# Block norm and router norm from one set of moments, with the order of the side tasks moved

## What is computed

```
attn   = softmax(s1) - sigmoid(lambda) * softmax(s2)         # causal
attn   = attn / max(sum(|attn|), 1e-6)
r1     = x + (attn @ v) @ Wo.T
x1     = (r1 - mean(r1)) / sqrt(var(r1) + 1e-5)              # block norm
xh     = (x1 - mean(x1)) * rsqrt(var(x1) + 1e-5)             # router norm
xn     = xh * gamma + beta                                   # to router and experts
probs  = softmax((xn @ router_w.T) / 1.5); top 2 of 8
moe    = sum over the top 2 of probs_e * (silu(xn @ W1[e]) @ W2[e])
out    = norm((moe + x1) + x1)                               # two residuals: 2 * x1
```

## Time and profile before

| | |
|---|---|
| runs | 1205.65, 1209.85, 1212.59 us; median 1209.85 |
| the profiled execution | 1201.04 us, of which the span of the trace is 1199.3 |
| busy share of the span | POOL 79%, PE 77%, DVE 77%, ACT 71% |
| costliest lines | L680 ACT exponentials 539.2 us, L962 DVE maxima 424.6, L614 POOL subtraction 406.5, L610 POOL scaling 312.4 |
| transfers | 139.39 MB, mean 116 GB/s over the span |
| mean granted clock of TensorE | 0.86 of full |

### The profile page before, as it was taken

One profiled execution on the slowest core, in us unless ns is written; L12 is line 12 of the kernel. 1 busy time (PEld: TensorE's weight loads), 2 busy tenths in 40 slices (PEclk: granted clock), 3 DMA queues, 4 the chain that ended last, 5 costly groups with the idle time before them and its releaser, 6 DMA issues.

```text
span 1199.3 us, 27952 instructions
## 1 busy us (share of the span) xinstructions
PE 927.8 (77%) x8522; PEld 738.7 (62%) x8522; DVE 924.3 (77%) x2393; ACT 851.7 (71%) x2706; POOL 948.1 (79%) x1257
## 2 busy tenths in 40 slices
PE   2588787868898788967799688977799787959582
PEld 1355564647676567846677466756578576748582
DVE  1588898859997799968997799968997689946242
ACT  1598987669887777868787777878788777853140
POOL 3399999898878997899878998799878898793402
PEclk9577788669998898989898898979998788978797
DMA  3703400533246524382235623382244632245662
GB/s 115 156 1 91 104 2 14 136 110 109 78 125 161 159 69 128 111 234 71 85 106 144 192 72 118 99 236 73 85 125 125 182 92 79 81 130 172 214 194 72
DMA packets 117046, 139.39 MB, mean 116 GB/s; under 512 B 11042, under 2 KB 99490, under 8 KB 116898
## 3 DMA queue, kind: packets, MB, share of 16 engines
q1 hardware_dynamic: 112802, 129.21, 37.4%
q0 software_dynamic: 4096, 8.40, 2.4%
HBM read 107.81 MB, written 29.75 MB: 115 GB/s over the span
## 4 chain that ended last, share of the span: by engine, by line
POOL 34%; DVE 22%; PE 19%; issue 12%; ACT 6%; DMA 5%; SPq 2%; DVEq 0%; POOLq 0%; ACTq 0%
POOL exps L614 13%; POOL exps L610 11%; DVE neg_max L962 7%; POOL x_sorted_dram L630 4%; PE trans L1124 4%; ACT exps L680 4%; POOL y_back L639 3%; DVE abs_sum L972 3%; PE scores L1090 3%; PE side L1067 3%; PE side L1073 3%; POOL lam_l L604 1%; DVE stats L760 1%; DMA xg<-x_sorted_dram 1%; DVE hT L924 1%
## 5 line engine op out<-in xcount | busy, mean ns | idle before, releaser
L680 ACT ACTIVATE exps<-scores,neg_max 128x512 f32<-128x512 f32 (+3 forms) x1024 | 539.2, 541 | 74.8 <-DVE neg_max L962 72.7
L962 DVE TENSOR_REDUCE neg_max<-scores 128x1 f32<-128x512 f32 (+3 forms) x896 | 424.6, 526 | 79.4 <-PE scores L1092 75.1
L614 POOL TENSOR_TENSOR exps<-exps 128x512 f32<-128x512 f32 x320 | 406.5, 1270 | 26.7
L610 POOL TENSOR_SCALAR exps<-exps,inv_l,lam_l 128x512 f32<-128x512 f32 (+3 forms) x512 | 312.4, 616 | 59.1 <-DVE inv_l L953 42.1
L1124 PE MATMUL trans<-ident,exps 128*128 128x128 f32 x1280 | 242.6, 320 | 148.4 <-POOL exps L614 114.0
L1124 PEld LDWEIGHTS trans<-ident,exps 128*128 128x128 f32 x1280 | 161.4, 160 | 216.3 <-POOL exps L614 169.6
L1090 PE MATMUL scores<-stack 72*128 72x512 bf16 (+3 forms) x1024 | 279.9, 343 | 15.5 <-DMA stack<-parts_dram 14.9
L972 DVE TENSOR_REDUCE abs_sum<-exps 128x1 f32<-128x512 f32 (+3 forms) x448 | 224.6, 525 | 67.6 <-POOL exps L614 67.2
L687 ACT ACTIVATE diffT<-trans 128x512 f32<-128x512 f32 x320 | 194.4, 608 | 95.2 <-PE trans L1124 93.8
L680 ACT ACTIVATION_READ_ACCUMULATOR exps<-scores,neg_max 128x1 f32 x1024 | 226.1, 221 | 0.0
L1092 PE MATMUL scores<-causal_bf,ident_bf 128*128 128x128 bf16 x1024 | 215.4, 243 | 0.0
(11 more groups left out here) (142 smaller groups left out, 871.9 us busy)
## 6 DMA issues: line engine op xcount, KB each, us to landing
w_sb<-w_dram SPq DMA_DIRECT2D x120, 512.0 KB, 3.7
stack<-parts_dram SPq DMA_DIRECT2D x288, 96.0 KB
parts_dram<-parts SPq DMA_DIRECT2D x104, 128.0 KB, 2.4
xg<-x_sorted_dram SPq DMA_DIRECT2D x24, 256.0 KB, 3.6
y_sorted_dram<-y_sorted SPq DMA_DIRECT2D x24, 256.0 KB, 3.8
x_in<-x_dram SPq DMA_DIRECT2D x8, 256.0 KB, 4.6
x_res<-x_dram SPq DMA_DIRECT2D x8, 256.0 KB, 4.6
o_dram<-y_out SPq DMA_DIRECT2D x8, 256.0 KB, 2.2
```

Of the source, the lines that this page charges most:

```text
L610: nc.gpsimd.tensor_scalar(diff[:, ring, col:col + w], exps[:, ring, 1, col:col + w], inv_l2[:, i:i + 1], lam_l1[:, i:i + 1], ALU.mult, ALU ...
L614: nc.gpsimd.tensor_tensor(diff[:, ring, :], diff[:, ring, :], exps[:, ring, 0, :], ALU.subtract)\
L680: nc.scalar.activation(exps[:, ring, k, col:col + w], scores[:, c % 2, k, col:col + w], ACT.Exp, bias=neg_max[:, c % 2, k, i:i + 1], accum ...
L962: nc.vector.tensor_reduce(neg_max[:, c % 2, k, i:i + many], scores[:, c % 2, k, col:col + many * w].rearrange("p (i w) -> p i w", w=w), AX ...
```

## The change

One set of moments serves both norms. With m and v the mean and variance of a row of `r1`, `x1` has mean 0 and variance v / (v + e), so the router norm of `x1` is (r1 - m) * (v (1 + e) + e^2)^-0.5, and twice `x1` is (r1 - m) * ((v + e) / 4)^-0.5. POOL makes both bases with one scale-and-add each over 128x4 and raises them in one power over 128x8, in task `out_proj`. Tasks `norm1` and `norm2` become one task `norms` at slot 18, in which DVE writes `x1_twice` and then `xh`, both straight from `r1` with four TENSOR_SCALAR each; `x1` is no longer made, and its moments and the 128x512 doubling are gone. The wait for the scatters of the batch before now stands between the two groups. The third norm uses the same functions; its epsilon is added by a constant instead of from the tile `eps_row`.

The order is moved too: `abs_sum` is taken five slots after its chunk instead of four (`LAG_DEN` follows it), `sorted` goes from slot 44 to 42, turn 2 from 58 to 59, y_out 1 and 2 a slot later, gather 2 and combines 0 and 1 a slot earlier, combines 2 and 3 a slot later, and the stores of the projections and the stack's loads (`PARTS_SLOT`, `STACK_SLOT`) a slot later.

```diff
@@ -55,7 +55,7 @@
-LAG_ABS = 4
+LAG_ABS = 5
 LAG_DEN = LAG_ABS + 1
-POST_SLOTS = {"spread": 8, "den_T": 10, "divide": 10, "out_proj": 12, "norm1": 16, "norm2": 18, "xn_T": 21, "logits": 22, "router_exp": 24, "count": 30, "place": 31, "sorted": 44, "norm3": 95, "finish": 98}
+POST_SLOTS = {"spread": 8, "den_T": 10, "divide": 10, "out_proj": 12, "norms": 18, "xn_T": 21, "logits": 22, "router_exp": 24, "count": 30, "place": 31, "sorted": 42, "norm3": 95, "finish": 98}
-TURN_SLOTS = (44, 52, 58, 68)
-Y_OUT_SLOTS = (57, 65, 72, 82)
+TURN_SLOTS = (44, 52, 59, 68)
+Y_OUT_SLOTS = (57, 66, 73, 82)
-GATHER_SLOTS = (82, 83, 85, 85, 86, 88, 89, 90)
-COMBINE_SLOTS = (86, 87, 88, 89, 90, 91, 92, 93)
-STACK_SLOT = 33
+GATHER_SLOTS = (82, 83, 84, 85, 86, 88, 89, 90)
+COMBINE_SLOTS = (85, 86, 89, 90, 90, 91, 92, 93)
+STACK_SLOT = 34
-PARTS_SLOT = 4
+PARTS_SLOT = 5
-        minus_half = sb("minus_half", [P, NT])
-        eps_row = sb("eps_row", [P, NT])
+        minus_half = sb("minus_half", [P, 2, NT])
-        x1 = sb("x1", [P, NT, D])
-        stats = sb("stats", [P, 3, NT, 6])
-        mv = sb("mv", [P, 3, NT, 2])
+        stats = sb("stats", [P, 2, NT, 6])
+        mv = sb("mv", [P, 2, NT, 2])
...
-        moments_done = signal("moments_done", 2)
+        moments_done = signal("moments_done", 1)
         eps_added = signal("eps_added", 2)
-        rstd_done = signal("rstd_done", 2)
+        rstd_done = signal("rstd_done", 1)
...
@@ -639,18 +635,22 @@
-                        if name in ("out_proj", "norm1", "norm3"):
-
-                            i = ("out_proj", "norm1", "norm3").index(name)
-                            moments, added, done = (moments_done, eps_added, rstd_done) if i < 2 else \
-                                (last_moments, last_eps, last_rstd)
-                            k = i + 1 if i < 2 else 1
-                            pool.wait_ge(moments.sem, moments.after(n, k))
-                            nc.gpsimd.tensor_tensor(var_eps[:, i, :], mv[:, i, :, 1], eps_row[:, :], ALU.add)\
-                                .then_inc(added.sem, 1)
-                            pool.wait_ge(added.sem, added.after(n, k))
-                            nc.gpsimd.tensor_tensor(rstd[:, i, :], var_eps[:, i, :], minus_half[:, :], ALU.pow)\
-                                .then_inc(done.sem, 1)
+                        if name == "out_proj":
+                            pool.wait_ge(moments_done.sem, moments_done.after(n, 1))
+                            nc.gpsimd.tensor_scalar(var_eps[:, 0, :], mv[:, 0, :, 1], EPS, 0.25, ALU.add, ALU.mult)\
+                                .then_inc(eps_added.sem, 1)
+                            nc.gpsimd.tensor_scalar(var_eps[:, 1, :], mv[:, 0, :, 1], 1.0 + EPS, EPS * EPS, ALU.mult, ALU.add)\
+                                .then_inc(eps_added.sem, 1)
+                            pool.wait_ge(eps_added.sem, eps_added.after(n, 2))
+                            nc.gpsimd.tensor_tensor(rstd[:, 0:2, :], var_eps[:, 0:2, :], minus_half[:, 0:2, :], ALU.pow)\
+                                .then_inc(rstd_done.sem, 1)
+                        if name == "norm3":
+                            pool.wait_ge(last_moments.sem, last_moments.after(n, 1))
+                            nc.gpsimd.tensor_scalar(var_eps[:, 2, :], mv[:, 1, :, 1], EPS, None, ALU.add)\
+                                .then_inc(last_eps.sem, 1)
+                            pool.wait_ge(last_eps.sem, last_eps.after(n, 1))
+                            nc.gpsimd.tensor_tensor(rstd[:, 2, :], var_eps[:, 2, :], minus_half[:, 0, :], ALU.pow)\
+                                .then_inc(last_rstd.sem, 1)
@@ -754,23 +754,19 @@
-            def moments(n, i, src):
+            def moments(i, src):
 
                 for t in range(NT):
                     nc.vector.bn_stats(stats[:, i, t, :], src[:, t, :])
                 nc.vector.drain()
                 for t in range(NT):
                     last = nc.vector.bn_aggr(mv[:, i, t, :], stats[:, i, t, :])
-                last.then_inc((moments_done if i < 2 else last_moments).sem, 1)
-
-            def normalise(n, i, dst, src):
-                if i < 2:
-                    dve.wait_ge(rstd_done.sem, rstd_done.after(n, i + 1))
-                else:
-                    dve.wait_ge(last_rstd.sem, last_rstd.after(n, 1))
+                return last
+
+            def normalise(dst, src, i, scale):
                 for t in range(NT):
                     last = nc.vector.tensor_scalar(dst[:, t, :], src[:, t, :], mv[:, i, t, 0:1],
-                                                   rstd[:, i, t:t + 1], ALU.subtract, ALU.mult)
+                                                   rstd[:, scale, t:t + 1], ALU.subtract, ALU.mult)
                 return last
@@ -865,18 +861,14 @@
-                            moments(n, 0, r1)
-                        if name == "norm1":
-                            normalise(n, 0, x1, r1).then_inc(x1_done.sem, 1)
-                            dve.wait_ge(x1_done.sem, x1_done.after(n, 1))
-                            moments(n, 1, x1)
-                        if name == "norm2":
-
+                            moments(0, r1).then_inc(moments_done.sem, 1)
+                        if name == "norms":
+
+                            dve.wait_ge(rstd_done.sem, rstd_done.after(n, 1))
+                            normalise(x1_twice[:, n % 2, :, :], r1, 0, 0).then_inc(acc_set.sem, 1)
                             if n:
                                 dve.wait_ge(scattered.sem, scattered.after(n - 1, TOP * NT))
-                            nc.vector.tensor_scalar(x1_twice[:, n % 2, :, :], x1[:, :, :], 2.0, None, ALU.mult)\
-                                .then_inc(acc_set.sem, 1)
-                            normalise(n, 1, xh, x1).then_inc(xh_done.sem, 1)
+                            normalise(xh[:, :, :], r1, 0, 1).then_inc(xh_done.sem, 1)
@@ -939,10 +931,11 @@
                                 op0=ALU.mult, op1=ALU.add).then_inc(combined.sem, 1)
                         if name == "norm3":
                             dve.wait_ge(combined.sem, combined.after(n, TOP * NT))
-                            moments(n, 2, acc)
+                            moments(1, acc).then_inc(last_moments.sem, 1)
                         if name == "finish":
                             dve.wait_ge(y_stored.sem, y_stored.after(n - 1, 1))
-                            normalise(n, 2, y_out, acc).then_inc(y_done.sem, 1)
+                            dve.wait_ge(last_rstd.sem, last_rstd.after(n, 1))
+                            normalise(y_out, acc, 1, 2).then_inc(y_done.sem, 1)
```

More of the change, by code:

```diff
@@ L299, in build @@
         side = [pb(f"side{n}", [P, 512]) for n in range(2)]
-        CONSTS = 21 + E
+        CONSTS = 20 + E
         weights_in = ctx.enter_context(nc.semaphore("weights_in"))
@@ L357, in build @@
         last_rstd = signal("last_rstd", 1)
-        x1_done = signal("x1_done", 1)
         acc_set = signal("acc_set", 1)
@@ L562, in _ @@
             nc.gpsimd.memset(ones_row[:, :], 1.0).then_inc(consts_made, 1)
-            nc.gpsimd.memset(minus_half[:, :], -0.5).then_inc(consts_made, 1)
-            nc.gpsimd.memset(eps_row[:, :], EPS).then_inc(consts_made, 1)
+            nc.gpsimd.memset(minus_half[:, :, :], -0.5).then_inc(consts_made, 1)
             for e in range(E):
```

## The result

The changed kernel takes 1212.55 us (median of 20 runs, 1207.55 to 1295.14), the kernel before 1206.39 in the same session (20 runs, 1196.93 to 1214.64): ratio 1.0052, interval 1.003 to 1.0074. Forecast were 1190 us and a gain; it is some 6 us slower. The run of 1295.14 us, alone at a mean granted clock of 0.63 where the others had about 0.85, is left out of the ratio.

The account below looks back on a forecast made before the run. The prediction took each batch to be bound by DVE in its first stretch and POOL in its second. Seven bodies times (1.4 + 1.4) plus 1 for the transfer gave about 20 us off 1209.85: 1190 us, range 1169 to 1209.

Parts of the forecast that it names:

- What bounds the kernel now: In a batch's first stretch the path runs mostly on DVE, in the second on POOL; no engine bounds alone.
- Norm1 on DVE: On DVE, 2.62 and 0.35 us go, a group of 1.6 (ends 1.05, 2.25) comes: 1.4 us gained per batch.
- The powers: On POOL at slot 14, the 128x8 power takes 1.84 us; POOL gains 0.2 us per batch, nothing on the path.
- abs_sum a slot later: DVE's waits at the end of slots 11 and 12 go, one in part: 1.4 us per batch (0.9 to 3.3).
- Moved slots: At slots 18 and 19, PE's projection wait goes and hidden 6 waits until about 727 us: both cost nothing.
- The transfer: On SP's queue, sorted ahead of weight 1 lets scatters land sooner: 1 us in all (ends 0 and 3).
- Tail: After the last body, 2.0 us gained from norm1 and norm2 and 2.0 lost on weight loading: nothing.
- The slow case: Burst at slot 19 held throughout, hidden 6 late behind it: 1.6 us per batch, 1221 us; chance 0.10.
- the gain is hidden: PE's waits for DVE end at ACT or its own work instead; some 3 us remain: 1207 us; chance 0.20.
- the larger rival: In DVE's stretch POOL's idle time fills, its 5.4 us of reciprocal waits go: 38 us, 1172 us; chance 0.17.

Follow-up runs that it names:

- extra16: The kernel before with four more 128x128 TENSOR_SCALAR on DVE in task norm1, into a tile nobody reads, nothing removed; ratio 1.0006 to the kernel before.
- norms_only: The change's arithmetic alone, with all tables and the abs_sum lag of the kernel before; ratio 1.0064 to the kernel before.

## Why the prediction was wrong

- **What bounds the kernel now** is the step that failed: "in the first stretch it runs mostly on DVE". That was read from DVE's share of a window and from `norm1` on the chain. The chain names one of two paths that were nearly level; POOL had 0.28 us of noted idle time in 25. Extra work of 1.45 us at that place cost nothing that can be told (extra16, 1.0006), and less work gained nothing (norms_only, 1.0064). DVE's 66.3 of 70 us count the time in which its instructions were held beside POOL's.
- **Norm1 on DVE.** 1.4 us a batch were credited as one sum. Its two halves lie on different sides of the handover: the 2.62 removed at slot 17 were covered, while the group added less the doubling (2.25 - 0.35 = 1.9) was in the exposed burst. The group took its upper end, 2.25, not 1.6. That is the end which the prediction gave to the rule of the Trainium skill that it cites (GPSIMD Engine Reference, section Specifications), and the trace agrees in this kernel, though not throughout: in `norms_only` it took 1.29. Where the holds fall changes with the burst's place against POOL, but the burst grew in both, from 4.6 us to 5.2 and 6.3. The lower end was read beside a power on POOL and not, as said, with POOL idle; with it idle a group lasts as long.
- **The powers.** 128x8 took 1.675 us where 1.84 was taken, so per batch POOL saved 0.37 us. No effect on the path was seen, as said, but the reason given, that DVE is the later engine there, falls with the first point; 0.37 x 7 is 2.6 us, less than most of these runs can tell.
- **abs_sum a slot later.** The waits went (11.3 us a batch to none in the list), and 9.0 us came back as waits for PE's scores (4.4 to 13.4). Alone the lag gives 0.9986; the 10 us (1.4 x 7, 0.992) that were taken lie outside its interval.
- **Moved slots.** `proj`'s wait for `xgT` went and hidden 6 came to stand for `rest`, as said, but it stood 4.22 us and began at 733.77, instead of at 727 at no cost. With turn 2 back at 58 the time is the same (1.0056 against 1.0052): so that standing is not the cause.
- **The transfer.** 1 us was credited for the scatters' landing. On the chain of after such landings take 5.48 and 6.77 us, where before's took 4.11 and 6.10, and ahead of the tail PE stands 9.8 us for the sorted tiles in both. No gain is seen.
- **Tail.** Costed at nothing. From the start of the last `r` to that of the last instruction into `xh` 8.8 us stand where 9.3 stood, 0.5 less and not over 3.
- **The start** was not in the sum: some 2 us by a tile's place in memory.
- **The rivals.** The slow case had the mechanism, a burst held throughout with hidden 6 behind it later than 728.6, and its size per batch was too large (1.6, against 0.5 to 0.7 in slots 12 to 20). It had a chance of 0.10, as the burst was expected to start 3 us earlier. It starts 1.8 us earlier, 21.3 us behind the first maxima of slot 12 instead of 23.1, and gives all of it back by its length and by hidden 6. That the gain is hidden, the rival at 0.20, is what happened to the 2.62 us, though behind POOL and not behind ACT or PE. POOL's waits for reciprocals, which the larger rival had going, stayed (5.4 and 5.5 us a batch).

## What to carry to other kernels

Before crediting work taken off an engine, look at the timeline of the engine that it waits for: if that one has no gap through the place, the work may well be covered, even where the chain runs through it, and adding the same work there once more tests it. Find the instruction at which the path changes engines, and keep apart what an edit removes ahead of it and what it adds behind it; here the same four instructions cost nothing that can be told in one slot and 10 us two slots further on. Fewer operations in all can be slower when the last ones left sit together in the exposed place.

## What the runs showed of the hardware

- A group of four 128x128 TENSOR_SCALAR on DVE takes 1.11 us where POOL is idle and 1.3 to 2.7 beside its chunks, and the holds in one burst are not additive: with 2.06 us put into it, it grew by 0.94.
- A power on POOL over 128x8 takes 1.675 us, over 128x4 1.02 to 1.04: an estimate of 0.16 us per element of the row, from these two shapes.
- A tile's place in memory, moved by 384 bytes, lengthened SP's issue of two stores from 1.50 to 1.97 us and their landing from 5.5 to 6.6 us, and delayed the first subtraction by 1.6 us.
- One kernel's tail took 14.5 us in one execution and 21.7 in another: 3.1 us more in steps between PE's instructions that the profile puts to "issue", and 4.1 more in the same matmuls, at a mean granted clock of 0.78 instead of 0.86.
